# A width-3 convolution computed as four outputs from six products in three sweeps, instead of two outputs from four products in two sweeps

## What is computed

```python
x = lax.conv_general_dilated(inputs, conv_w, window_strides=(1,), padding='SAME',
                             dimension_numbers=('NWC', 'WIO', 'NWC')) + conv_b   # inputs (2, 2048, 1024), conv_w (3, 1024, 768)
q, k, v = jnp.split(x, 3, axis=-1)
...                                # attention in blocks of 128 tokens, 16 heads, causal inside a block
x = _layernorm(x + attention @ proj_w + proj_b)
x = _layernorm(x + ffn(x))
```

## Time and profile before

| | |
|---|---|
| three runs | 1756.16, 1756.53, 1757.09 us (median 1756.53) |
| profiled execution, span | 1757.0 us (it has no other time on record) |
| TensorE matmul / weight load busy | 97% / 87% |
| VectorE / ScalarE / GpSimd busy | 74% / 39% / 19% |
| DMA traffic | 123.04 MB, mean 70 GB/s |
| convolution block | about a third of the span |

### The profile page before, as it was taken

One profiled execution on the slowest core, in us unless ns is written; L12 is line 12 of the kernel. 1 busy time (PEld: TensorE's weight loads), 2 busy tenths in 40 slices (PEclk: granted clock), 3 DMA queues, 4 the chain that ended last, 5 costly groups with the idle time before them and its releaser, 6 DMA issues. The chain is left out here.

```text
span 1757.0 us, 32959 instructions
## 1 busy us (share of the span) xinstructions
PE 1702.0 (97%) x11968; PEld 1532.1 (87%) x11968; DVE 1298.4 (74%) x3089; ACT 678.1 (39%) x1817; POOL 328.2 (19%) x272
## 2 busy tenths in 40 slices
PE   6899999999999899999999999989999999999998
PEld 5899999999999778888888888869999898999887
DVE  8977679987677566666666666777787887878785
ACT  4333324332333466766767766761111111111110
POOL 5200003400000100100101002053333333333331
PEclk9999999999999899999999999999999999999999
DMA  4323223332234200110110102141212111121211
GB/s 142 115 80 96 80 82 108 127 114 78 79 95 156 102 1 10 40 48 0 48 48 0 48 22 79 64 137 47 77 54 81 54 68 66 61 73 54 81 39 49
DMA packets 48805, 123.04 MB, mean 70 GB/s; under 512 B 5488, under 2 KB 13680, under 8 KB 48240
## 3 DMA queue, kind: packets, MB, share of 16 engines
q1 hardware_dynamic: 48752, 122.36, 21.2%
HBM read 88.79 MB, written 33.55 MB: 70 GB/s over the span
## 5 line engine op out<-in xcount | busy, mean ns | idle before, releaser
L388 PE MATMUL conv_acc<-x_split,weights 128*128 128x256 f32 x4608 | 557.8, 284 | 30.9 <-DVE weights L314 23.5
L388 PEld LDWEIGHTS conv_acc<-x_split,weights 128*128 128x128 f32 x4608 | 554.8, 191 | 33.6 <-DVE weights L314 25.2
L1315 PE MATMUL ps_f<-weights 128*128 128x266 f32 (+2 forms) x1728 | 329.5, 343 | 0.0
L1315 PEld LDWEIGHTS ps_f<-weights 128*128 128x128 f32 x1728 | 277.4, 189 | 23.9
L247 ACT ACTIVATE x_split<-x_mixed 128x1024 fp32r<-128x1024 f32 x128 | 135.7, 1060 | 308.2 <-PE conv_acc L388 278.7
L309 DVE TENSOR_TENSOR x_split<-x_mixed,x_split 128x1024 fp32r<-128x1024 f32 x128 | 158.7, 1240 | 100.5 <-ACT x_split L247 100.5
L803 DVE CUSTOM_DVE_ANT_0 scores_and_probs<-ps_scores,causal_mask 128x128 f32<-128x128 f32 x512 | 118.6, 287 | 127.6 <-PE ps_scores L923 123.8
L710 ACT ACTIVATE scores_and_probs<-scores_and_probs,score_neg_max 128x128 f32<-128x128 f32 x512 | 197.9, 391 | 4.8 <-DVE score_neg_max L808 4.7
L1151 ACT ACTIVATE gate_exp<-h_and_gate,gate_neg_max 128x8 f32<-128x8 f32 x32 | 9.6, 301 | 348.5 <-DVE gate_neg_max L1226 348.5
L676 POOL TENSOR_TENSOR weights<-conv_tile,weights 128x1024 fp32r<-128x1024 f32 x14 | 35.7, 2551 | 439.1 <-ACT weights L696 353.9
L1315 PE MATMUL ps_f<-late_weights,weights 128*128 128x266 f32 (+2 forms) x576 | 116.1, 337 | 0.0
(11 more groups left out here) (115 smaller groups left out, 2423.1 us busy)
## 6 DMA issues: line engine op xcount, KB each, us to landing
x_raw<-in_xT SPq DMA_DIRECT2D x128, 257.0 KB, 2.7
conv_tile<-in_x SPq DMA_DIRECT2D x32, 512.0 KB, 3.4
out<-out_tile SPq DMA_DIRECT2D x32, 512.0 KB, 2.7
convT_scratch<-features_out SPq DMA_DIRECT2D x16, 768.0 KB, 3.5
conv_tile<-convT_scratch SPq DMA_DIRECT2D x16, 768.0 KB, 6.3
conv_w_raw<-in_conv_w SPq DMA_DIRECT2D x16, 576.0 KB, 4.0
weight_stage<-in_ffn_w SPq DMA_DIRECT2D x8, 581.0 KB, 3.7
yT_scratch<-features_out SPq DMA_DIRECT2D x8, 512.0 KB, 3.7
```

What stands on the lines that cost most here:

```text
L388: last = nc.tensor.matmul(acc[f][k // 2][:, k % 2, :], w[:, c, a, k, f * P:(f + 1) * P], xs[:, c % XS, b, k, :], start=(c == 0 and k % 2 = ...
L1315: mm = nc.tensor.matmul(ps_f[par][n][:, 0:b0 - a0], x1T[:, par, a, kc, :], wf[kc][:, b, a0:b0], start=(kc == 0 and k == 0), stop=(n == 2 a ...
```

## The change

Six products now give four outputs. A unit is 1024 tokens, four phases of 256 (token number modulo 4), and all 6 feature groups at once. A sweep does 2 of the 6 products for 4 units; there are 3 sweeps, 12 units. A unit has 4 granules (j counts them, 0 to 47) of 2 chunks each; a granule is 72 matmuls of the same form as before.

- Sweep 0 uses taps 0 and 2 as they are (load of 2 taps, no mixing). Sweeps 1 and 2 mix three taps on VectorE (`mix_weights`), in place; GpSimd mixes nothing any more. The two raw weight buffers lie in memory that is used later by attention. The arena holds one sweep's weights, so a chunk's weights are overwritten after TensorE's last use in the sweep before.
- x is loaded as 1 MB granules in sweeps 0 and 1, into two buffers. Two more planes, needed in sweep 2 (ce), are made in granules 4 to 15 and 28 to 31, stored to DRAM and loaded back.
- ScalarE takes a unit's sums out in three pairs of banks (`evacuate`). Those of sweep 0 go to DRAM (on ScalarE's DMA queue), those of sweep 1 are added and subtracted by VectorE (`finish_first`) and go to DRAM, those of sweep 2 are combined with both (`finish_second`, eight operations for a pair) into four phases of output and stored to convT.
- The phases are stored in an order by which each block of 128 tokens is permuted; the mask rows, x of the residual and the output are permuted likewise (masks by GpSimd and four small DMAs, the rest on the host).
- Nothing in the convolution is a loop any more; all of it is written out. TensorE waits at the end of each unit for its own last matmul before it counts the granule as used.

The diff, cut; lines of "..." are left out. `stt` is VectorE's scalar_tensor_tensor; CPG is 2, GRAN 4, FP 3, NU 4.

```diff
-XS = 4
+XS = 3
...
+    SW = 3
+    U = SW * NU
+    J = GRAN * U
+    ST_E = FP * NU
...
+    CE_FIRST = (4, 28)
...
+    def pieces(j):
+        return [(u, p) for u in range(NU, U) for p in range(FP) if GRAN * u + 6 + p == j]
...
+            def load_x(j):
+                if j >= 2:
+                    sp.wait_ge(x_mix, j - 1)
+                sp.dma_start(xraw[j % 2], xT[n_of[j // GRAN], j % GRAN]).then_inc(x_loaded[j % 2], 16)
+            def load_w(n):
+                if n >= 2:
+                    sp.wait_ge(w_lo, n - 1)
+                if n < CC:
+                    sp.dma_start(wraw[n % 2][:, 0:TAPS:2, :], conv_w[n % CC][:, 0:TAPS:2, :]).then_inc(w_loaded[n % 2], 16)
+                else:
+                    sp.dma_start(wraw[n % 2], conv_w[n % CC]).then_inc(w_loaded[n % 2], 16)
...
+            def load_planes(j):
+                q = ce_source(j)
+                sp.wait_ge(x_lo, j - 1)
+                sp.wait_ge(ce_stored[q % 2], 16 * (q // 2 + 1))
+                sp.dma_start(T[:, j % 2, 0:3:2], ce_dram[q]).then_inc(t_loaded[j % 2], 16)
...
+                load_x(j)
+                if ce_index(j - 2) is not None:
+                    store_ce(j - 2)
+                for u, p in pieces(j - 3):
...
+                if 18 <= j < 18 + GRAN - 1:
+                    load_w(CC + CPG * (j - 17))
+                    load_w(CC + CPG * (j - 17) + 1)
...
+            for j in range(2 * GRAN * NU, J):
+                load_planes(j)
+                if j < 2 * GRAN * NU + 1 + GRAN - 1 and j > 2 * GRAN * NU:
+                    load_w(2 * CC + CPG * (j - 32))
+                    load_w(2 * CC + CPG * (j - 32) + 1)
...
+                for u, p in pieces(j - 2):
+                    if u < 2 * NU:
+                        store_sd(u, p)
+                if j == 36:
+                    load_attn_w(attn.WV)
...
+            load_l(U - 2, 2)
+            store_y(U - 2, 0)
+            load_l(U - 1, 0)
+            store_y(U - 2, 1)
+            load_attn_w(attn.WQ)
+            load_l(U - 1, 1)
+            store_y(U - 2, 2)
+            load_attn_w(attn.WK)
+            load_attn_w(attn.WO)
+            load_l(U - 1, 2)
+            for p in range(FP):
+                store_y(U - 1, p)
...
+            def split_x(j):
+                act.wait_ge(x_mix, j + 1)
+                if j >= XS:
+                    act.wait_ge(x_used, j - XS + 1)
+                nc.scalar.activation(xs[:, j % XS, HI], T[:, j % 2, 0:2], ACT.Copy).then_inc(x_hi, 1)
...
-                    unit(u, None, sweep)
-                unit(NST * (sweep + 1) - 1, None, sweep, sweep == SWEEPS - 1)
-            copy_mid(LAST_UNIT, SWEEPS - 1)
+                    act.wait_ge(w_mix, n - CC + 1)
+                    act.wait_ge(x_used, GRAN * NU * s - GRAN + c // CPG + 1)
+                nc.scalar.activation(w[:, c, HI], wraw[n % 2][:, 0:TAPS:2, :], ACT.Copy).then_inc(w_hi, 1)
...
+            def evacuate(u, pairs=range(FP)):
+                s = u // NU
+                for p in pairs:
+                    e = FP * u + p
+                    act.wait_ge(acc_done, e + 1)
...
+                        dst, k = m[e % 2], e - ST_E
+                        if k < 2:
+                            act.wait_ge(m_stored[k], 16 * ST_E // M_COUNT)
+                        else:
+                            act.wait_ge(m_free, k - 1)
+                    for f in range(2):
+                        bank = acc[2 * p + f]
...
+                            last = nc.scalar.activation(dst[:, f], bank[:], ACT.Copy, scale=1.0 / 24.0)
+                    last.then_inc(evac, 1)
+                    if s == 0:
+                        act.wait_ge(evac, e + 1)
+                        act.dma_start(m_dram[n_of[u], p], dst).then_inc(m_stored[e % M_COUNT], 16)
...
+            for j in range(J):
+                split_x(j)
+                if j < GRAN:
+                    for n in range(CPG * j, CPG * j + CPG):
+                        split_weights(n)
+                before = j >= GRAN + 1 and j % GRAN == 1
+                if before:
+                    evacuate(j // GRAN - 1, range(FP - 1))
+                for s in range(1, SW):
+                    g = j - (GRAN * NU * s - 1)
+                    if 0 <= g < GRAN:
+                        for n in range(CPG * g, CPG * g + CPG):
+                            split_weights(CC * s + n)
+                if before:
+                    evacuate(j // GRAN - 1, range(FP - 1, FP))
+            split_attn(attn.WV, J - 3)
+            split_attn(attn.WQ, J - 2)
+            split_attn(attn.WK, J - 2)
+            act.wait_ge(attn.c_loaded, 32)
+            act.wait_ge(x_used, J - 1)
+            for a, b in (attn.V, attn.K, attn.Q):
+                nc.scalar.activation(attn.cs[:, HI, a:b, :], attn.craw[:, a:b, :], ACT.Copy).then_inc(attn.c_hi, 1)
+            evacuate(U - 1)
...
+            def mix(j):
+                t, s = T[:, j % 2], sweep_of(j)
+                if j >= 2:
+                    dve.wait_ge(x_lo, j - 1)
+                if s == 2:
+                    dve.wait_ge(t_loaded[j % 2], 16 * ((j - 2 * GRAN * NU) // 2 + 1))
+                    first = step(stt(t[:, 1], t[:, 2], -2.0, t[:, 0]), "x", x_step)
+                    dve.wait_ge(x_step, first)
+                    stt(t[:, 0], t[:, 2], 2.0, t[:, 0]).then_inc(x_mix, 1)
+                    return
+                dve.wait_ge(x_loaded[j % 2], 16 * (j // 2 + 1))
...
+                if s == 0:
+                    a = step(stt(t[:, 0], d[2], -5.0, d[4]), "x", x_step)
+                    b = step(stt(t[:, 1], d[3], -5.0, d[5]), "x", x_step)
...
+                    step(stt(t[:, 0], d[2], -4.0, d[4]), "x", x_step)
+                    a = b = step(stt(t[:, 2], d[1], -4.0, d[3]), "x", x_step)
...
+                if q is not None:
...
+                    nc.vector.tensor_tensor(ce[q % 2][:, 0], d[4], d[2], ALU.subtract)
...
+                if s == 0:
+                    stt(t[:, 0], t[:, 0], 0.25, d[0])
+                    dve.wait_ge(x_step, b)
+                    stt(t[:, 1], d[1], 4.0, t[:, 1]).then_inc(x_mix, 1)
+                else:
+                    c = step(nc.vector.tensor_tensor(t[:, 1], t[:, 0], t[:, 2], ALU.subtract), "x", x_step)
+                    dve.wait_ge(x_step, c)
+                    nc.vector.tensor_tensor(t[:, 0], t[:, 0], t[:, 2], ALU.add).then_inc(x_mix, 1)
...
+            def mix_weights(n):
+                r = wraw[n % 2]
+                dve.wait_ge(w_loaded[n % 2], 16 * (n // 2 + 1))
+                if n < 2 * CC:
+                    a = step(nc.vector.tensor_tensor(r[:, 2, :], r[:, 0, :], r[:, 2, :], ALU.add), "w", w_step)
+                    dve.wait_ge(w_step, a)
+                    b = step(nc.vector.tensor_tensor(r[:, 0, :], r[:, 2, :], r[:, 1, :], ALU.add), "w", w_step)
+                    dve.wait_ge(w_step, b)
...
+            def finish_first(u, p):
+                e = FP * (u - NU) + p
+                dve.wait_ge(evac, FP * u + p + 1)
...
+                nc.vector.tensor_tensor(dst[:, :, 0, :], a[:, :, 0, :], a[:, :, 1, :], ALU.add)
+                nc.vector.tensor_tensor(dst[:, :, 1, :], a[:, :, 0, :], a[:, :, 1, :], ALU.subtract).then_inc(m_free, 1)
+                dve.wait_ge(m_free, e + 1)
+                dve.sem_inc(fin_done, 1)
...
+            def finish_second(u, p):
+                e = FP * (u - 2 * NU) + p
+                dve.wait_ge(evac, FP * u + p + 1)
...
+                else:
+                    dve.wait_ge(y_stored[e % 2], 32 * (e // 2))
...
+                y2 = step(nc.vector.tensor_tensor(y[2], a[:, :, 0], a[:, :, 1], ALU.add), "f", fin_step)
+                nc.vector.tensor_tensor(y[1], a[:, :, 0], a[:, :, 1], ALU.subtract).then_inc(m_free, 1)
+                dve.wait_ge(l_loaded[e % 2], 32 * (e // 2 + 1))
+                dve.wait_ge(fin_step, y2)
+                y0 = step(nc.vector.tensor_tensor(y[0], y[2], s, ALU.add), "f", fin_step)
+                dve.wait_ge(m_free, ST_E + e + 1)
+                y3 = step(stt(y[3], y[1], 8.0, d), "f", fin_step)
+                dve.wait_ge(fin_step, y0)
+                stt(y[2], y[2], 4.0, s)
+                dve.wait_ge(fin_step, y3)
+                stt(y[1], y[1], 2.0, d)
+                nc.vector.tensor_tensor(y[0], y[0], m0, ALU.add)
+                nc.vector.tensor_tensor(y[3], y[3], m5, ALU.add).then_inc(fin_done, 1)
...
+            for j in range(J):
+                new = [CC * s + CPG * (j - GRAN * NU * s + 1) + i for s in range(1, SW)
+                       if 0 <= j - (GRAN * NU * s - 1) < GRAN for i in range(CPG)]
+                early = GRAN <= j < 2 * GRAN * NU - 1
+                if early:
+                    mix(j + 1)
+                for u, p in pieces(j):
+                    finish(u, p)
+                for n in new:
+                    mix_weights(n)
+                split_x(j)
+                if j < GRAN:
+                    new = list(range(CPG * j, CPG * j + CPG))
```

(72 more changed lines are left out.)

482 lines of the change are left out of this document (248 added, 234 removed).

## The result

| | before | after |
|---|---|---|
| median (lowest to highest), 4 runs each | 1756.35 us (1756.03 to 1757.09) | 1654.98 us (1654.62 to 1655.36) |
| profiled execution, span | 1757.0 us | 1652.8 us |
| convolution's last matmul ends | 588.6 us | 463.4 us |
| attention starts on TensorE | 592.1 us | 488.3 us |

What follows compares the result with a forecast made beforehand. Bound by the count of matmuls, except where a sweep's weights are made. Start 15.9, matmuls 409.4, sweep changes 25 and unit ends 3 give 453.3; attention starts at 474.8 instead of 592.1, -117.3: 1639 us, range 1616 to 1674.

Steps and rivals of the forecast that it cites:

- Matmuls: TensorE, convolution block: 3456 matmuls of the same form instead of 4608, at 118.5 ns each, 409.4 us, -136.5.
- if matmuls have another pace: TensorE's timeline: a sign that the prediction is wrong, as it expected long runs at 118.5 ns a matmul.
- Unit ends: TensorE's wait for its own last matmul, 12 times: 0.25 us each, bounds 0 and 0.5, 3 us in all.
- VectorE keeps up: VectorE's work per granule stays below TensorE's 8.53 us in each sweep, so it is hidden.
- Start: Unit 0: TensorE starts at 13.0 us instead of 9.4; loss 15.9 instead of 30.5.
- Sweep changes: Granules 16 and 32: stalls for the last bank pair's copy, 10.4 and 14.6 us with +3 clock each; 25 instead of 12.3.
- What is late next is ready in time: After the sweep-change stalls: x of granules 18 and 34 is ready in time because TensorE was held before.
- Tail: Block's end: TensorE starts attention 20 us after the last matmul instead of 3.5, bounds 10 and 30; clock another 1.5.
- (c): Rival: DMA becomes the bound outside the sweep changes too, at 200 GB/s; +60, 1700 us; chance 8%.
- (e): Rival: DRAM round trips hold the whole block to 185 GB/s, slower than before, 1797 us; chance 3%.
- below 330 GB/s outside the starts of sweeps: DMA windows in the convolution block: expected to stay under this rate, a sign that would show the forecast.
- rival (d): Code fetch in the loop-free block: 30 instruction packets each hold TensorE up 2.7 us, +81, 1720 us; chance 3%.

Runs made afterwards that it cites:

- the last kernel above: Changed kernel with unit-end, copy-order, tail and bias-wait edits, plus a third raw weight buffer and earlier mixing of three chunks per sweep change: 1610.92 us, ratio 0.9167.

## Why the prediction was right, and what it mis-sized

**Matmuls.** The count, 3456, held and carries the result. The pace of 118.5 ns was taken from rows 2 and 3 and was 120.0: 3456 x 1.5 = +5.2 us. This step failed by "of the same form": shape and count per row are the same, the pace isn't quite, and "if matmuls have another pace" was one of the prediction's own signs of being wrong. No edit changed it, not the wait, the order nor the DMA traffic. Nor is it the missing loop: in the kernel before, units 0 and 8 were written out, and where they run without waits they keep the same 118.3 ns as the looped ones. Its cause is open, and layout or access pattern of the operands, which the change also altered, was not tried.

**Unit ends.** Taken at 0.25 within bounds of 0 and 0.5; they are 0.54 each (0.46 longer to the next start, 0.07 to the one after), above the bound. The row it was taken from, a matmul's record of 0.28 us, is close to the 0.30 that the trace shows as idle, not to what the wait costs. The 11 inside the block come to 6.1 instead of 3.0 (two follow a small wait for ScalarE besides).

**VectorE keeps up.** Right, at its prices: 512 columns took 687 ns, 768 took 958, 1536 took 1754 as records, each some 0.1 us less from start to start. No gap in the middle of a sweep. GpSimd had nothing to do in the block.

**Start.** 14.4 for 13.0, the table load of 1.28 us on the path. It stood at 0.74 before, and the wait for the bias was not looked at as something that could move it. Unit 0 loses 16.6 in all (15.9 predicted): the clock at the start and the 0.17 wait at granule 3 are less than feared.

**Sweep changes.** The place, the bank pair and the releaser were right. Pauses 7.9 for 7.4 and 13.6 for 11.6. The clock, by windows after the second pause (columns as above):

```profile
322.00:324.00 2.00, 0.00 (x0) 0.00 (x0) 0.51 (x1) 1.40 (x5) 0.00 (x0) 0.50 0.88 244
324.00:326.00 2.00, 1.96 (x9) 1.96 (x10) 0.28 (x1) 0.94 (x1) 0.00 (x0) 0.50 0.87 332
...
328.00:330.00 2.00, 2.00 (x16) 2.00 (x15) 1.80 (x3) 1.30 (x1) 0.00 (x0) 0.78 0.03 14
```

The granted clock is 0.50, 1.2 GHz instead of 2.4; 21 matmuls then lie 213 ns apart instead of 120. With the first's 0.26 that is 2.2 us, 1.8 after the first pause; 3 each was predicted. From start to start each pause is 0.16 longer than its idle time. Together 9.9 and 15.9, without the unit ends, for 10.4 and 14.6. "What is late next is ready in time" held for the kernel as it is, just: with the copies earlier, x of granules 18 and 34 was next.

**Tail.** 24.9 for 20. Its steps in the timeline of the changed kernel, VectorE, ScalarE and SyncE:

```profile
442.75 0.35 SPq L256 DMA_DIRECT2D weight_stage<-in_attn_w  x1
...
450.70 1.92 ACT L399 ACTIVATE weights<-weight_stage 128x2048 fp32r<-128x2048 f32 x1 [10.30 <-DMA weight_stage<-in_attn_w]
...
460.35 1.91 ACT L399 ACTIVATE weights<-weight_stage 128x2048 fp32r<-128x2048 f32 x1 [7.73 <-DMA weight_stage<-in_attn_w]
...
481.84 0.69 DVE L528 TENSOR_TENSOR x_raw<-conv_m 128x512 f32<-128x512 f32 x1 [4.22 <-DMA convT_scratch<-x_raw]
...
486.06 0.68 DVE L540 TENSOR_TENSOR x_raw<-x_raw 128x512 f32<-128x512 f32 x1
```

Loads of WQ and WK, taken at 4.8, were used 8.0 and 5.4 after their issue (442.75 to 450.70; 454.97 to 460.35): the first shares the engines with 1 MB stores and loads of partial sums. And the last sums waited 4.2 for the store of the first, taken at 1. These three are 7.0 more than predicted; the rest of the tail was some 2 shorter. The errors are one: a duration measured where little else was moved, used where transfers overlap. The extra 1.5 for the clock did not come: from attention's start to the end it is 1164.6 us, before 1164.9.

**DMA.** 113 MB forecast in the block, 248 GB/s x 449 us = 111. It was hidden, up to a share of 0.95 in the window from 60 to 100 us; rivals (c) and (e) fell. That window moved 358 GB/s, so the sign "below 330 GB/s outside the starts of sweeps" did not hold, and cost nothing. The page on issues shows the price of that load, which nobody had to pay outside the changes and the tail (KB each, median us to landing):

```profile
x_raw<-in_xT SPq DMA_DIRECT2D x32, 1028.0 KB, 6.8
...
conv_tile<-in_conv_w SPq DMA_DIRECT2D x8, 1152.0 KB, 6.7
weight_stage<-in_conv_w SPq DMA_DIRECT2D x8, 1152.0 KB, 9.0
```

**Code.** There are 47 packets of instructions, 0.77 MB, against 30 and 0.49. All gaps of TensorE in the block have another releaser, and the last kernel above has none at all: rival (d) fell. By the rule of the Trainium skill (Runtime: NRT & Kernel Launch, Instruction fetch mechanics), straight code is fetched ahead and mostly hidden; the trace agrees.

**The sum.** Start +0.7, pace +5.2, unit ends +3.1, changes +0.8 (-0.5 and +1.3), block's end 463.4 for 453.3 with the last matmul's 0.3; tail +4.9, clock -1.5 and 0.3 less behind it. Spans: -104.2 for -117.3. The other 2.7 us or so lie in the yardstick: nearly every other execution, of either kernel, takes 1.8 more than its span, so before's profiled one (span 1757.0) took about 1758.8, 2.3 more than the median it was set against, while after's (1654.62) is 0.4 less than its own. The range's lower end, 1616, does not take the tail's -10 that it names; with it and the unit ends at 0 it would be 1605. Nothing hangs on it here.

## What to carry to other kernels

Where one engine feeds another through two buffers, walk the loop load, compute, write, load at the point where work of that kind begins: here 27 us hung on it. Another order of copies took some of it, and a third buffer with an earlier start all but 0.2 of what was left, without one operation less. When a transfer is costed, take its duration from a stretch that is as full as the one it will run in. Order edits are worth their wait only up to the next limit: find that one before counting the gain. And before a loss is put down to an edit, look whether it lies before the edit's first effect: with more DMA traffic, most of it did.

## What the runs showed of the hardware that was not expected

- TensorE's wait for its own last matmul costs 0.54 us, though the trace shows 0.30 of idle time: four units merge into one row without it.
- Matmuls of 128 x 128 by 256 columns start 120.0 ns apart on average in this kernel, and 115 to 123, 118.3 on average, in the one before. Open.
- The activation table's load, 1.28 us, sat at 8.59 us with the wait for the bias ahead of ScalarE's first operation, and at 0.74 when that wait was moved. In the Trainium skill (ScalarE: Activation LUTs, What ACT_TABLE_LOAD costs) the load is 1283 ns, and each switch to another set costs a drain of about 1380 ns besides. The first figure agrees. Of the second nothing is seen at this load, the kernel's first: the first activation starts 0.20 us after it.
- DMA shares of 0.93 to 1.01 left matmuls at 120 ns.
